# Row maxima of attention: turned by VectorE in 32x32 blocks and moved by DMA, instead of turned by TensorE and copied by ScalarE

## The reference

```python
qkv = hidden_states @ qkv_w + qkv_b
q = _rope(q, cos, sin); k = _rope(k, cos, sin)
scores = jnp.einsum('bqhd,bkhd->bhqk', q, k) * scale
scores = scores + (1.0 - causal) * MASK_VAL
probs = jax.nn.softmax(scores, axis=-1)
ctx = jnp.einsum('bhqk,bkhd->bqhd', probs, v)
```

## Time and profile before

| | |
|---|---|
| median of 3 runs | 611.6 us (611.2 to 612.4) |
| profiled execution, its own time | 611.91 us |
| its span, first to last instruction | 610.0 us |
| PE busy | 590.7 us (97%) |
| DVE busy | 383.0 us (63%) |
| ACT busy | 290.2 us (48%) |
| POOL busy | 386.2 us (63%) |
| chain that ended last | PE 79% of the span |
| slots 0 to 39 of the first pass start at | 37.99 to 154.32 us |
| slots 0 to 39 of the second pass start at | 246.48 to 362.06 us |

### The profile page before, as it was taken

One profiled execution on the slowest core, in us unless ns is written; L12 is line 12 of the kernel. 1 busy time (PEld: TensorE's weight loads), 2 busy tenths in 40 slices (PEclk: granted clock), 3 DMA queues, 4 the chain that ended last, 5 costly groups with the idle time before them and its releaser, 6 DMA issues.

```text
span 610.0 us, 9847 instructions
## 1 busy us (share of the span) xinstructions
PE 590.7 (97%) x3368; PEld 424.7 (70%) x3368; DVE 383.0 (63%) x912; ACT 290.2 (48%) x448; POOL 386.2 (63%) x598
## 2 busy tenths in 40 slices
PE   6999999999999999999999999999999999999996
PEld 5876666666677887666666666788887676767664
DVE  5986778666427489877786663366985261516257
ACT  3625777556734622276766566354122453232432
POOL 6896956656435578878575555348979594821363
PEclk9999999999999999999999999999999999999999
DMA  9788776654512237658577554942600000000002
GB/s 302 236 303 251 208 212 189 195 139 103 145 54 87 87 103 220 210 165 250 148 216 223 154 160 130 353 157 95 238 5 1 1 0 2 0 1 1 0 30 109
DMA packets 60369, 83.63 MB, mean 137 GB/s; under 512 B 17936, under 2 KB 26768, under 8 KB 60320
## 3 DMA queue, kind: packets, MB, share of 16 engines
q1 hardware_dynamic: 57968, 75.02, 41.2%
q10 hardware_dynamic: 2352, 8.00, 3.4%
HBM read 65.17 MB, written 26.99 MB: 151 GB/s over the span
## 4 chain that ended last, share of the span: by engine, by line
PE 79%; DMA 5%; DVE 3%; issue 3%; POOL 3%; ACT 3%; SPq 2%; POOLq 0%; ACTq 0%; DVEq 0%
PE proj_ps L1004 9%; PE proj_ps L1006 7%; PE proj_ps L1005 7%; PE ctx_ps L1161 5%; PE score_ps L1034 4%; PE proj_ps L1209 4%; PE proj_ps L1210 3%; PE scoreT_ps L1043 3%; PE score_ps L1004 2%; PE score_ps L1006 2%; PE score_ps L1005 2%; PE scoreT_ps L1004 2%; PE scoreT_ps L1006 2%; PE scoreT_ps L1005 2%; PE ctx_ps L1209 2%
## 5 line engine op out<-in xcount | busy, mean ns | idle before, releaser
L821 POOL TENSOR_TENSOR w_lo<-raw,w_hi 128x512 fp32r<-128x512 f32 x98 | 132.3, 1355 | 64.7 <-ACT w_hi L1374 59.2
L1555 DVE CUSTOM_DVE_ANT_0 score_ps<-score_ps,causal 128x512 f32<-128x512 f32 (+3 forms) x256 | 118.9, 522 | 60.7 <-PE score_ps L1034 60.5
L1423 ACT ACTIVATE probs_T<-scoreT_ps 128x1024 f32<-128x1024 f32 x80 | 82.2, 1027 | 46.1 <-PE scoreT_ps L1043 45.0
L1004 PE MATMUL proj_ps<-xn_hi,w_hi 128*128 128x512 f32 x224 | 96.8, 432 | 1.6 <-ACT by_sin L1352 1.2
L1006 PE MATMUL proj_ps<-xn_lo,w_hi 128*128 128x512 f32 x224 | 88.5, 395 | 0.0
L1005 PE MATMUL proj_ps<-xn_hi,w_lo 128*128 128x512 f32 x224 | 88.5, 395 | 0.0
L852 POOL TENSOR_SCALAR_AFFINE_SELECT probs_T<-probs_T 128x256 f32<-128x256 f32 x128 | 55.5, 457 | 14.2 <-ACT probs_T L1423 14.1
L1004 PEld LDWEIGHTS proj_ps<-xn_hi,w_hi 128*128 128x128 f32 x224 | 42.0, 188 | 26.6 <-issue 14.4
L1333 ACT ACTIVATE q_st<-one_turn_ps 2x512 fp32r<-2x512 f32 x64 | 37.5, 587 | 32.5 <-PE one_turn_ps L1020 32.1
L979 POOL TENSOR_TENSOR hsL<-hidden_T,hsH 128x256 fp32r<-128x256 f32 x44 | 37.6, 872 | 23.4 <-ACT hsH L1495 22.9
L1006 PEld LDWEIGHTS proj_ps<-xn_lo,w_hi 128*128 128x128 f32 x224 | 42.2, 188 | 10.0
(11 more groups left out here) (317 smaller groups left out, 1348.6 us busy)
## 6 DMA issues: line engine op xcount, KB each, us to landing
raw<-w SPq DMA_DIRECT2D x98, 256.0 KB, 2.8
rows<-rows_hi SPq DMA_DIRECT2D x32, 256.0 KB, 3.8
arranged<-tern SPq DMA_DIRECT2D x96, 85.0 KB
q_st<-rows SPq DMA_DIRECT2D x32, 200.0 KB
k_st<-rows SPq DMA_DIRECT2D x32, 200.0 KB
rows<-rows_lo SPq DMA_DIRECT2D x16, 256.0 KB, 4.3
gate_w<-arranged ACTq DMA_DIRECT2D x4, 704.0 KB, 7.2
up_w<-arranged ACTq DMA_DIRECT2D x4, 704.0 KB, 8.3
```

Of the source, the lines that this page charges most:

```text
L821: nc.gpsimd.tensor_tensor(w_lo[n % SPLIT][:, :], raw[n % RAW][:, :], F32(w_hi[n % SPLIT][:, :]), ALU.subtract).then_inc(unit_ready, 1)
L1004: nc.tensor.matmul(acc, lh, rh, start=first, stop=False)
L1423: nc.scalar.activation(probs_T[g % 2][x][:, :, :], scoreT_ps[:, :, :], ACT.Exp, scale=0.25).then_inc(probs_ready, 1)
L1555: m = nc.vector.tensor_tensor_reduce(out=block, in0=block, in1=causal[:, S - w:], scale=1.0, scalar=-3e38, op0=ALU.add, op1=ALU.max, accum ...
```

## The change

The turn of the row maxima leaves TensorE, GpSimd and (as a copy) ScalarE. VectorE splits the maxima itself, turns them in 32x32 blocks into rows of a new buffer `max_rows` (32 partitions by 512), and ScalarE's queue issues two transfers of 2 rows of 512 to `q_st`. The splitting stands behind the row maxima of slots 5g + 2 and 5g + 4 (the high part) and at the end of these slots (the low part); the four block transposes stand in slot 5g + 3 or 5g + 5 behind the row maxima of the next task. `scores_T` waits for the landing of the transfers. `deal()` drops the cost of the turn (22) and tops slots up to 215 instead of 230; by its arithmetic nine slots of each pass get another number of triples, most of them one more or one fewer (slots 14, 15, 20, 24, 25, 38, 39, 41 and 42), and the running sum is never off by more than one or two. The rounded copy of the identity goes, and `max_cols` has one buffer instead of two.

```diff
-    held = [43 * (...) + 33 * (...) + 22 * (max_in(s) is not None) + 53 * (...)
+    held = [43 * (...) + 33 * (...) + 53 * (...)
...
-        while len(at) < TRIPLES and (room >= triple / 2 and at.count(s) < 3 or held[s] + triple * at.count(s) < 230):
+        while len(at) < TRIPLES and (room >= triple / 2 and at.count(s) < 3 or held[s] + triple * at.count(s) < 215):
...
 GpSimd, each slot:
-                    if max_in(s) is not None:
-                        join_maxima(b, max_in(s))
...
 TensorE, each slot:
-                            pe.wait_ge(*copied(b, ("max", 2 * g + x // 2)))
+                            pe.wait_ge(max_stored, 32 * (PAIRS * b + 2 * g + x // 2 + 1))
...
-                    if max_in(s) is not None:
-                        max_turn(b, max_in(s))
...
 ScalarE:
             def max_out(b, j):
-                n, g = use(b, ("max", j)), GROUPS * b + j // 2
-                act.wait_ge(turned, n + 1)
+                n, g = PAIRS * b + j, GROUPS * b + j // 2
+                act.wait_ge(max_turned, n + 1)
                 for hh in range(2):
-                    m = nc.scalar.activation(q_st[g % 3][64 * hh:64 * hh + 2, j % 2, :], turn_bank(n)[32 * hh:32 * hh + 2, :], ACT.Copy)
-                m.then_inc(turn_done(n), 1)
+                    act.dma_start(F32(q_st[g % 3][64 * hh:64 * hh + 2, j % 2, :]), max_rows[2 * hh:2 * hh + 2, :]).then_inc(max_stored, 16)
...
 VectorE:
+            def round_maxima(b, j):
+                n = PAIRS * b + j
+                maxima = row_max[:, j % 2, :].rearrange("p (t h) -> p t h", t=NT)
+                hi = max_cols[:, :, 0:4:2]
+                dve.wait_ge(part_ready, TASKS * b + PARTS * (j // 2) + (3, 5)[j % 2])
...
+                    dve.wait_ge(max_turned, n)
+                nc.vector.tensor_copy(hi, maxima).then_inc(max_hi, 1)
+            def rest_of_maxima(b, j):
...
+                dve.wait_ge(max_hi, n + 1)
+                nc.vector.tensor_tensor(lo, maxima, F32(hi), ALU.subtract).then_inc(max_ready, 1)
+            def turn_maxima(b, j):
+                n = PAIRS * b + j
+                dve.wait_ge(max_ready, n + 1)
+                if n:
+                    dve.wait_ge(max_stored, 32 * n)
+                for r in range(NT):
+                    m = nc.vector.transpose(max_rows[:, :].rearrange("p (t r i) -> p r t i", t=NT, r=4)[:, r], F32(max_cols[32 * r:32 * r + 32, :, :]))
+                m.then_inc(max_turned, 1)
...
-            dve.wait_ge(ident_in, 16)
-            nc.vector.tensor_copy(ident_r[:, :], ident[:, :]).then_inc(ident_rounded, 1)
...
                     if score_in(s):
                         row_maxima(b, s)
+                        g, x = score_in(s)
+                        if x in (2, 4):
+                            round_maxima(b, 2 * g + x // 4)
+                    if max_in(s) is not None:
+                        turn_maxima(b, max_in(s))
...
+                    if max_in(s + 1) is not None:
+                        rest_of_maxima(b, max_in(s + 1))
```

More of the change, by code:

```diff
@@ L181, in deal @@
 def deal():
-    held = [43 * (score_in(s) is not None) + 33 * (prob_in(s) is not None) + 22 * (max_in(s) is not None) + 53 * (ctx_in(s) is not None)
+    held = [43 * (score_in(s) is not None) + 33 * (prob_in(s) is not None) + 53 * (ctx_in(s) is not None)
             + (sum((14, 86, 64, 43, 22)[kt + 1] for kt in (-1, *pv_in(s)[1])) if pv_in(s) else 0) for s in range(SCORE_SLOTS)]
@@ L339, in program @@
     rope_sin = sb("rope_sin", [P, S], f32)
-    at[0] += E * 4
+    max_rows = sb("max_rows", [32, S], f32)
     out_bias = sb("out_bias", [P, E], f32)
@@ L385, in program @@
     at[0] += 30720
-    max_cols = sb("max_cols", [P, 2, NT, 34], f32r)
+    max_cols = sb("max_cols", [P, NT, 32], f32r)
     o_h = at[0]
@@ L484, in program @@
     ident_in = sem("ident_in")
-    ident_rounded = sem("ident_rounded")
     v_used = sem("v_used")
@@ L520, in program @@
     max_ready = sem("max_ready")
+    max_turned = sem("max_turned")
+    max_stored = sem("max_stored")
     scoreT_done = sem("scoreT_done")
@@ L830, in rope_lo @@
                 nc.gpsimd.tensor_tensor(rows_lo[t][:, :], turned_rows[t][:, :], F32(rows_hi[t][:, :]), ALU.subtract).then_inc(rows_lo_ready, 1)
[L832 to L844, removed]
             def keep_causal(b, s):
@@ L907, in _ @@
                     if b == 0 and u == 1:
-                        nc.gpsimd.memset(F32(max_cols[:, :, :, :]), 0.0).then_inc(cols_set, 1)
+                        nc.gpsimd.memset(F32(max_cols[:, :, :]), 0.0).then_inc(cols_set, 1)
                 if b:
@@ L1010, in unit @@
                 return w_hi[n % SPLIT], w_lo[n % SPLIT]
-            def max_turn(b, j):
-                pe.wait_ge(max_ready, PAIRS * b + j + 1)
-                if PAIRS * b + j == 0:
-                    pe.wait_ge(ident_rounded, 1)
-                n = use(b, ("max", j))
-                if TURN_BANK[n][1]:
-                    pe.wait_ge(turn_done(n), TURN_BANK[n][1])
-                for qt in range(NT):
-                    m = nc.tensor.matmul(turn_bank(n)[0:34, qt * P:(qt + 1) * P], max_cols[:, j % 2, qt, :], ident_r[:, :], start=True, stop=True)
-                m.then_inc(turned, 1)
             def stacks(b, j, hh):
@@ L1557, in row_maxima @@
                 m.then_inc(part_ready, 1)
+            def round_maxima(b, j):
[3 more added lines that the diff above has]
+                dve.wait_ge(part_ready, TASKS * b + PARTS * (j // 2) + (3, 5)[j % 2])
+                if n == 0:
+                    dve.wait_ge(cols_set, 1)
+                else:
+                    dve.wait_ge(max_turned, n)
+                nc.vector.tensor_copy(hi, maxima).then_inc(max_hi, 1)
+            def rest_of_maxima(b, j):
+                n = PAIRS * b + j
+                maxima = row_max[:, j % 2, :].rearrange("p (t h) -> p t h", t=NT)
+                hi, lo = (max_cols[:, :, x:4:2] for x in range(2))
+                dve.wait_ge(max_hi, n + 1)
+                nc.vector.tensor_tensor(lo, maxima, F32(hi), ALU.subtract).then_inc(max_ready, 1)
+            def turn_maxima(b, j):
+                n = PAIRS * b + j
+                dve.wait_ge(max_ready, n + 1)
[4 more added lines that the diff above has]
+                m.then_inc(max_turned, 1)
             def norm_stats(k):
```

2 lines of the change are left out of this document (removed).

## The result

The changed kernel takes 647.3 us (median of 4 runs, 642.3 to 657.8) against 611.4 for the kernel before on the same chip; the ratio is 1.056, with a 95% interval of 1.050 to 1.062. The forecast was 612 us with a range of 603 to 621. It is wrong: the change loses 34 us by the ratio, 36 by the medians.

What follows compares the result with a forecast made beforehand. The prediction took TensorE to bound every window, by a thin margin over VectorE. TensorE's saving of 11.4 us and an equal loss to VectorE's added work gave 611.9 - 11.4 + 11.4 = 611.9, stated as 612 us, range 603 to 621.

Steps and rivals of the forecast that it cites:

- the size of the landing: ScalarE's transfers to `q_st`: 4 KB lands 2.2 us after issue under load, so `scores_T` waits nothing.
- rival 2: Late landings: `scores_T` waits 0.3 us or more a pair, 2.8 us a pass, 617.5 us in all; chance 0.20.
- The 2.0 us: Fixed cost of a transfer whatever its size, from the Trainium skill; at it the landing wait is nothing as well.
- What TensorE saves: Turns leaving TensorE: 24 at 0.23 us and 8 at 0.73 with the bank wait, 11.4 us in all.
- GpSimd and the identity: Two small GpSimd instructions a pair and the rounded identity (1.00 us on VectorE at the start) go: counted as nothing.
- The new deal at nothing: The changed `deal()` moves single triples by a slot and changes no sum: nothing by itself.
- VectorE's price: Six added VectorE instructions a pair: transposes 0.96 us, roundings 0.2 and 0.1; 1.26 us a pair, 40 in all.
- the small waits for it: New TensorE waits at `score_ps` for row maxima and at `proj_ps` for VectorE: some 4 to 5 us a pass.
- the give-back: The added work takes back all 11.4 us that TensorE saves, leaving 0 over both passes.
- the 612 of the sum: Whole kernel: 611.9 - 11.4 + 11.4 = 611.9 us, stated as 612.
- The carried windows: Five-slot stretches of a pass worked through with the added VectorE work: changes from -0.7 to +1.4 us, summing to 0.0.
- ScalarE's issue: Each transfer issue on ScalarE takes 0.33 to 0.53 us; two issues (0.9) replace two copies (1.19): even.

Runs made afterwards that it cites:

- the run with the scratch: Changed kernel, transposes and new deal kept, transfers sent to a DRAM scratch, scores not waiting for them (maxima not subtracted): 612.3 us, ratio 0.999.
- relief, old deal: Changed kernel without transposes, transfers and their wait (roundings stay), deal() back at 22 for a turn and bound 230: 600.0 us, ratio 0.980.
- with transposes, old deal: Changed kernel, transfers to a DRAM scratch and no wait for them, deal() back at 22 for a turn and bound 230: 610.8 us, ratio 0.999.

## Why the prediction was wrong, by its own steps

**The step that failed** is the size of the landing: "Less the moving of such a size, 2.2 for 4 KB under load." It measured 2.77 us in the median over the 32 turns, from 1.67 to 5.49, and 1.69 with the traffic taken away. The wait that this makes was to be "nothing" and is 25.0 us. The mechanism stood there as rival 2, at a chance of 0.20, and even its 2.8 us is the median of the landings, but its price was worked out from that one number as 0.3 us a pair, 617.5 in all. Two things are missing from it. The landing is late by turns: of the 25.0 us, 19.8 are waits of 1.1 to 3.2 us in eight slots (5, 17, 27 and 32 of each pass), where SyncE had issued row reads, row writes or copies in the microseconds before., medians over transfers of 256 KB, could not show it. The order of SyncE's issues around each turn would have given a warning. And six of the long waits are followed by over 3 us each at half the clock, 10 us in all, for which the prediction has no term. The 2.0 us that the prediction names beside this are given in the Trainium skill, "DMA: Bandwidth & Descriptors", section "Anatomy of one DMA — SWDGE (gpsimd) path", for transfers issued from GpSimd. These were issued from ScalarE, and the quickest landed in 1.67.

**What TensorE saves**: 11.4 us predicted, 611.9 to 600.0 measured with the old deal. Right within 0.5 us for everything that was taken away. That GpSimd and the identity, counted at nothing, are worth nothing was not measured apart.

**The new deal at nothing** ("moves single triples by a slot and changes no sum"): wrong. It costs 4.5 us where VectorE has only the roundings added, some 1.5 with the transposes, gains 1.4 in the kernel before, and keeps some landings from being later still: without it the changed kernel is 12 us slower by the ratios.

**VectorE's price**: the transposes take 0.299 us and stand 0.31 apart, 1.24 us a pair instead of 0.96, the upper end of the prediction. The roundings take 0.17 each where nothing disturbs them, but 0.32 and 0.36 on average. The lines by source (ns min, median, max):

```profile
L1555 DVE STREAM_TRANSPOSE max_rows<-max_cols x128: 294/299/304, 48.7 to 401.0; 32x128 f32<-32x128 f32 x128
...
L1537 DVE CAST max_cols<-row_max x32: 172/173/1262, 46.6 to 399.1; 128x8 fp32r<-128x8 f32 x32
...
L1302 ACTq DMA_DIRECT2D q_st<-max_rows x64: 569/570/1172, 49.9 to 401.9; - x64
```

With 38.3 us of transposes, 10.3 and 11.3 of roundings that is 60 us on VectorE instead of 40 (its busy time grew by 50, from 383.0 to 433.0). It is above 90% busy in slots 18 to 22 (15.90 of 16.95), as foreseen, and the small waits for it are 4.4 us a pass in the changed kernel and 6.7 in the run with the scratch, where 4 to 5 were foreseen. Yet the give-back was predicted at 11.4 and measured at 10.8: the 612 of the sum is met by the run without the wait, by errors that cancel. The carried windows show where they lie. The times between the starts of the scores five slots apart, second pass, in us, from the timelines of PE:

| slots | before | predicted | relief, old deal | with transposes, old deal | with transposes, new deal | changed kernel |
|---|---|---|---|---|---|---|
| 3 to 7 | 14.39 | +0.5 | 14.03 | 15.44 | 15.39 | 18.07 |
| 8 to 12 | 16.69 | +0.4 | 16.61 | 18.15 | 18.21 | 19.12 |
| 13 to 17 | 14.92 | -0.6 | 13.88 | 13.87 | 13.97 | 18.20 |
| 18 to 22 | 15.25 | +1.4 | 14.86 | 15.43 | 16.14 | 16.95 |
| 23 to 27 | 14.41 | -0.3 | 13.90 | 14.59 | 13.96 | 18.92 |
| 28 to 32 | 14.96 | -0.7 | 13.83 | 14.08 | 14.09 | 16.27 |
| 33 to 37 | 14.21 | -0.5 | 13.18 | 13.99 | 13.97 | 14.13 |

The sixth column is what the prediction was about, and its signs are right in every window. The two windows from slot 3 to slot 12 lose 1.0 and 1.5 us, together 1.6 more than predicted. Slots 18 to 22 lose 0.9 instead of 1.4, and only 0.2 with the old deal. Slots 13 to 17 gain 0.9 instead of 0.6, and the last three windows gain 1.6 together, about what they were given. From the sixth column to the last the landings' waits and the clock behind them are added, 2.2 to 5.0 us in the four windows with the longest waits.

**ScalarE's issue**: 0.57 us, above the 0.33 to 0.53 of the rows, so the second transfer goes out 0.12 later than carried. That is a small part of waits of up to 3 us.

## What to carry to other kernels

A small transfer on which the bound engine waits is to be priced at what other queues have in flight when it is issued, turn by turn, and not at one median or at its size (here 1.67 to 5.49 us for the same 4 KB): read the issues of every queue in the few microseconds before each of them. A long wait of TensorE costs more than itself, for its clock can fall to half behind it. And before calling an edit of the work's order free, run it alone: here it was worth from -1.4 to 4.5 us, and 12 in company.

## What was not expected of the hardware

**VectorE beside GpSimd.** Ten of the 64 small roundings (128 partitions x 8 numbers) took 0.94 to 1.26 us instead of 0.17, each while a two-operand instruction of GpSimd ran, and each ended about when that did:

```profile
333.65 1.26 POOL L819 TENSOR_TENSOR w_lo<-raw,w_hi 128x512 fp32r<-128x512 f32 x1
333.70 1.24 DVE L1537 CAST max_cols<-row_max 128x8 fp32r<-128x8 f32 x1
```

The Trainium skill, "SBUF — State Buffer", section "SBUF: two separate sides", says that VectorE and GpSimd share one pair of ports, which VectorE needs with two SBUF inputs or in a two-port mode, and that the one that comes second is blocked for the whole instruction. The trace agrees for the low part, with its two inputs. Four of the ten are the CAST, with one input; whether it ran in such a mode no row shows. The transposes were not held up: 28 of the 128 ran wholly beside a two-operand instruction of GpSimd, and none took longer than 0.304 us.

**The clock.** In the changed kernel six of the seven waits for a landing that were over 2 us (2.09, 2.33, 2.83, 3.01, 3.02 and 3.15) were followed by windows at a granted clock of 0.50; the seventh (2.28) was not, nor was one of 1.97 for key rows. The kernel before, with no wait over 0.8 us in its slots, has a mean clock of 1.000. Waits for VectorE did the same: both of 2.0 us in the run without transposes and transfers were followed by over 3 us at 0.50. What sets the seventh apart was not looked into by a run.
